# A decoder layer in 16 pipelined groups: one order table replaced by another, with begins of its own for each of six stages

## The reference

```python
h = rms_norm(x, g_pre)                                  # sublayer 1: gated recurrence
a = sigmoid(bit_linear(h, w_a) + decay_bias); i = sigmoid(bit_linear(h, w_i)); v = bit_linear(h, w_v)
rec = chunked_scan(a, sqrt(clip(1 - a*a, 1e-8)) * (i * v))      # state = a * state + input
x1 = layernorm(2*x + rec + bit_linear(silu(bit_linear(rms_norm(rec, g_post), w_gate)), w_down))
Q, K = rope(x1 @ Wq.T + bq), rope(ctx @ Wk.T + bk); V = ctx @ Wv.T + bv     # sublayer 2: 16 heads of 16
x2 = layernorm(x1 + softmax(where(mask == 0, min, Q @ K.T / 4)) @ V @ Wo.T + bo)
y = relu(s0 * concat(x2, -x2) @ (+-1)[k0]) * 2                  # sublayer 3: 512 -> 1024 -> 1024 -> 256
y = s2 * (relu(s1 * y @ (+-1)[k1]) * 2) @ (+-1)[k2]
out = layernorm(x2 + y)
```

## Time and profile before

| | |
|---|---|
| median of 3 runs | 890.84 us (889.0 to 891.39) |
| profiled execution | 888.45 us, of which its span is 886.7 us |
| PE busy | 800.9 us |
| DVE busy | 642.4 us |
| ACT busy | 549.2 us |
| POOL busy | 296.9 us |
| DMA | 57.47 MB, mean 65 GB/s |

### The profile page before, as it was taken

How to read it: one execution, slowest core, us unless ns; L and a number is a source line. 1 busy time by engine, 2 the same in 40 slices (tenths; PEclk the granted TensorE clock), 3 DMA queues, 4 the chain that set the end, 5 groups by cost and what they waited for, 6 DMA issues and landing times.

```text
span 886.7 us, 17907 instructions
## 1 busy us (share of the span) xinstructions
PE 800.9 (90%) x6856; PEld 626.3 (71%) x6890; DVE 642.4 (72%) x1224; ACT 549.2 (62%) x917; POOL 296.9 (33%) x476
## 2 busy tenths in 40 slices
...
DMA packets 52517, 57.47 MB, mean 65 GB/s; under 512 B 7856, under 2 KB 48848, under 8 KB 49360
## 3 DMA queue, kind: packets, MB, share of 16 engines
...
## 4 chain that ended last, share of the span: by engine, by line
PE 61%; DVE 16%; ACT 9%; DMA 4%; issue 4%; POOL 3%; SPq 1%; DVEq 0%; ACTq 0%; POOLq 0%
PE bankC L1118 18%; PE bankA L1053 6%; PE bankC L1102 6%; PE bankA L987 6%; PE slotB L1021 6%; PE slotB L1040 5%; PE bankA L922 5%; DMA q_st<-m_lo 4%; DVE u L1304 2%; ACT pr L794 2%; PE bankA L903 2%; DVE bn L1359 2%; ACT sqT L682 2%; ACT L794 2%; POOL rstd L574 2%
## 5 line engine op out<-in xcount | busy, mean ns | idle before, releaser
L1118 PE MATMUL bankC<-h0h,w 128*128 128x256 f16 x1024 | 233.7, 273 | 0.6 <-DVE h0l L1452 0.5
L1118 PE MATMUL bankC<-h0l,w 128*128 128x256 f16 x1024 | 233.3, 272 | 0.0
L1408 DVE TENSOR_REDUCE nmax<-slotB 128x4 f32<-128x1024 f32 x128 | 150.7, 1216 | 1.8 <-PE slotB L1021 0.3
L794 ACT ACTIVATE pr<-slotB 128x1024 f32<-128x1024 f32 x128 | 127.5, 1028 | 13.3 <-PE slotB L1040 13.0
L1118 PEld LDWEIGHTS bankC<-h0h,w 128*128 128x128 f16 x1024 | 99.9, 98 | 15.2 <-issue 1.2
L1118 PEld LDWEIGHTS bankC<-h0l,w 128*128 128x128 f16 x1024 | 100.1, 98 | 14.2
L1040 PE MATMUL slotB<-q_st,k_st 99*128 99x256 bf16 x512 | 74.7, 274 | 13.4 <-DMA q_st<-m_lo 11.2
L573 POOL TENSOR_SCALAR rstd<-mv 128x2 f32<-128x2 f32 x48 | 9.3, 193 | 215.6 <-DVE mv L1362 214.5
L1021 PE MATMUL slotB<-k_st,q_st 97*128 97x256 bf16 x512 | 76.7, 272 | 4.2 <-DVE nmax L1408 2.5
L1040 PEld LDWEIGHTS slotB<-q_st,k_st 99*128 99x128 bf16 x512 | 43.9, 97 | 38.3 <-DMA q_st<-m_lo 15.9
L1102 PE MATMUL bankC<-xh,w 128*128 128x256 f16 x256 | 57.8, 273 | 14.3 <-DVE xl L1446 13.7
...
## 6 DMA issues: line engine op xcount, KB each, us to landing
k_st<-scr SPq DMA_DIRECT2D x96, 128.0 KB, 4.5
q_st<-scr SPq DMA_DIRECT2D x96, 128.0 KB, 4.3
...
```

The costliest lines, as they stand in the source:

```text
L794: act.activation(pr[i % 2][:, c, :, :].rearrange("p h s -> p (h s)"), slotB[ringB.slot(g, name)][:, :], ACT.Exp, scale=DH ** -0.5).then_in ...
L1118: ins = pe.matmul(bankC[ringC.slot(g, name)][:, e * T:(e + 1) * T], w_1[:, i // 2, (2 * m + e) * P:(2 * m + e + 1) * P], (h0h, h0l)[i % 2] ...
L1408: dve.tensor_reduce(nmax[:, hg * HG * NT + n:(hg + 1) * HG * NT:NT], slotB[ringB.slot(g, name)][:, :].rearrange("p (h s) -> p h s", s=S), ...
```

## The change

The one table `TIMES` with the one list `BEGIN` becomes seven tables. Steps belong to `weights` or to one of six stages (recurrent, keys, queries, scores, values, network), each with its own list of begins; `when(step, engine, g)` takes the begin of the step's stage. From group 4 to group 12 all six lists advance by 47.87 in each group; in the first and the last groups they differ. Numbers of all steps are new, and with them the order on every engine and the places in the rings. No step's code, wait, buffer or DMA is changed: keys and queries still go to DRAM and back.

```diff
-TIMES = """
-    w:s V-601.472 P-451.567 | w:m V-188.378 A-211.738 P-145.016 | w:a V-131.916 | w:iv V-41.444
...
-BEGIN = [0, 53.194, 106.603, 159.927, 213.209, 266.528, 319.858, 373.172, 426.486, 479.8, 533.114, 586.428, 639.742, 693.116, 746.368, 799.574]
+TIMES = {
...
+    "scores": """
+        score0 P93.89 V95.551 | score1 P94.556 V101.441 | score2 P96.349 V103.898 | score3 P99.631 V104.717
...
+BEGIN = {
+    "weights": [0],
+    "recurrent": [0, 51.387, 91.429, 137.718, 185.585, 233.451, 281.317, 329.184,
+                  377.05, 424.917, 472.783, 520.649, 568.516, 616.394, 664.2, 712.324],
...
+    "scores": [0, 36.554, 83.319, 130.981, 178.847, 226.714, 274.58, 322.446,
+               370.313, 418.179, 466.046, 513.912, 561.778, 609.722, 657.92, 704.956],
...
 ENGINES = ("PE", "ACT", "DVE", "POOL", "SP")
...
+AT, BEGINS = times()
+
+
+def when(step, engine, g):
+    return BEGINS[step][g] + AT[step][engine]
 
 
 def order(engine):
 
-    steps = [(BEGIN[g] + at[engine], n, step, g)
-             for n, (step, at) in enumerate(AT.items()) if engine in at
-             for g in range(1 if step.startswith("w:") else G)]
+    steps = [(when(step, engine, g), n, step, g)
+             for n, (step, at) in enumerate(AT.items()) if engine in at for g in range(len(BEGINS[step]))]
     return [(step, g) for _, _, step, g in sorted(steps)]
...
-        for start, name, g in sorted((BEGIN[g] + AT[name]["PE"], name, g) for name in items for g in range(G)):
+        for start, name, g in sorted((when(name, "PE", g), name, g) for name in items for g in range(G)):
             engine, last = items[name]
             s = until.index(min(until))
             self.where[(name, g)] = (s, n[s])
-            until[s] = BEGIN[g] + AT[last][engine]
+            until[s] = when(last, engine, g)
             n[s] += 1
```

94 lines of the change are left out of this document (57 added, 37 removed).

## The result

The change makes the kernel 1.2% faster, by less than half of what was forecast: 880.88 us median (879.02 to 882.22) against 891.12 us for the kernel before, measured beside it; ratio 0.9878, 95% interval 0.9861 to 0.9896. The profiled execution took 882.22 us with a span of 880.3 us. Lines of the new program are those of the old plus 31.

A forecast was written before the change was run, and what follows sets the result against it. TensorE, 90% busy, was taken as the bound. Pitch 49.5 - 2.65 + 0.5 = 47.35 us gives 27.6 us less over 12.85 groups; fill +5.6, drain -5, together -27.0: 861.4 profiled, 864 median, range 849 to 882.

The forecast's parts named there:

- The three waits: TensorE's steady-part waits for xl, the row of maxima in q_st and sqT: 2.65 us a group, forecast to go.
- the drain: From l0_0(13) to l0_0(15): the old waits go there too, 5 us less, between 2 and 8.
- the last network: Group 15's network alone at the end, 31.0 us, same order in both kernels.
- rival 2: SyncE's queue delivers the row of maxima late in every group; at 6.5 us late about 920 us; chance 8%.
- One of the three readings: At sqT before down: only exp1.0 (0.44 us) stood between them in the old order; its 0.6 us wait goes.
- new small waits, 0.5 us: Steady part, each group: the new order's small delays cost 0.5 us, bounds 0 and 1.3.
- rival 1: VectorE becomes the bound between score0 and max: pitch 48.5 us, 880 us; chance 16%.
- the walk: One group followed through all five queues of the new order with the trace's durations; the fill was walked too.
- the ten places that come out 0.1 to 0.2 us late: Steps late in one steady group, x2T among them: 1.3 us added up, taken as 0.5.
- VectorE needs 18.9 us ... PE's order has 19.9 us: From score0 to max in each group: VectorE's work fits TensorE's matmuls with 0.3 us to spare.
- the fill, +5.6 us: Start until l0_0(0): the new order reaches it at 135.5 us, against 129.9 for equal work, 6 us either way.

The follow-up runs named there:

- Experiment 16: Changed kernel with GpSimd's rotk working on 8 of 256 columns from group 2 on, so keys are wrong: 868.78 us, ratio 0.9738 to the kernel before.
- 17: Changed kernel with round3's multiplication and rounding of sg on ScalarE instead of VectorE, whole computation: 870.54 us, ratio 0.9776 to the kernel before.
- experiment 3: Changed kernel with VectorE's maximum of xg (scale) behind x2 instead of ahead of the third maximum: 890.92 us, ratio 0.9998 to the kernel before.
- 4: Changed kernel with SyncE sending the query parts (qput) before gathering the key stack (kget): 911.97 us, ratio 1.024 to the kernel before.
- 8: Changed kernel with three of six key-stack gathers fetching one row instead of sixteen from group 2 on: 875.17 us, ratio 0.9824 to the kernel before.
- 10: Changed kernel with VectorE's two operations on the key parts ahead of layer 0's first low half: 887.68 us, ratio 0.9965 to the kernel before.
- 9: Changed kernel with the last low half of layer 1 behind x2 on VectorE: 895.71 us, ratio 1.006 to the kernel before.
- 11: Changed kernel with seven idle_work blocks left out and five added in earlier gaps of the fill: 876.88 us, ratio 0.9833 to the kernel before.
- 12: Changed kernel with layer 1's last low half behind x2, key parts ahead of layer 0's low half, and idle_work blocks moved: 896.79 us, ratio 1.0064.
- 15: Changed kernel with score5 later on PE, round3 ahead of score4's maximum, two maxima later on VectorE, and idle_work blocks moved: 880.0 us, ratio 0.9886.
- 14: Changed kernel with score5 later on PE, round3 ahead of score4's maximum and two maxima later on VectorE: 883.97 us, ratio 0.9937 to the kernel before.
- 18: Changed kernel with round3's multiplication on ScalarE and idle_work blocks moved in the fill, whole computation: 866.27 us, ratio 0.972 to the kernel before.
- 1: Changed kernel with each maximum reading only the first 128 of 256 keys: 869.96 us, ratio 0.9776 to the kernel before.
- 2: Kernel before, old order, with each maximum reading only the first 128 of 256 keys: 883.94 us, ratio 0.993 to the kernel before.
- 6: Changed kernel with x2T behind l2.2 and l2.3 and v ahead of the maxima on PE: 885.62 us, ratio 0.9936 to the kernel before.

## Why the prediction was off

**Right.** The three waits of the earlier trace rows are gone and came back nowhere as such. TensorE was the engine to follow, the drain gave 6.0 us for the 5 forecast, the last network took 30.9 us, and the row of maxima in SyncE's queue (rival 2) didn't decide. The direction was right. One of the three readings was wrong, though its wait went: between sqT and down the old order had not exp1.0 alone but also two quarter-steps of layer 1, 2.2 us in all and more than the new order's 1.75. What made sqT late was ScalarE's list, with a table load (1.28 us) and an exponential ahead of it, and that is what the new order took away:

```profile
440.17 1.28 ACT L794 ACT_TABLE_LOAD   x1 [1.88 <-PE slotB L1040]
441.46 1.02 ACT L794 ACTIVATE pr<-slotB 128x1024 f32<-128x1024 f32 x1
442.38 1.11 ACT L682 ACTIVATE sqT<-bankA,cst 128x1024 bf16<-128x1024 f16 x1
```

The time lies in the range of 849 to 882 us, 1.1 us from its end, and the forecast of 864 missed by 16.9.

**Wrong: the term "new small waits, 0.5 us".** It measured 1.54 us, over even its upper bound of 1.3; in 12.85 groups that is 13 us of the 17 missed. With it the pitch is 49.5 - 2.65 + 1.54 = 48.4, as measured, so the rest of that sum was right. The mechanism is that of rival 1, VectorE between score0 and max, which had been given 16%; its number (pitch 48.5, 880 us) fits by luck. Its own terms, 1.3 us and as much again, give 49.4, and the 0.9 that it then takes off comes from no row; and it had the fill at 5.6 us. x2T stood in the walk among the ten places that come out 0.1 to 0.2 us late; it waits 0.77. Two steps of the working failed.

First, the step "VectorE needs 18.9 us ... PE's order has 19.9 us". It took round3 at 1.25 us, its duration beside an idle GpSimd; in the new order it takes 0.69 + 0.17 + 1.58 = 2.44 us beside rotk. With these 1.2 us the step's own sum is 0.9 us short where it had 0.3 to spare. Experiment 16 takes the neighbour away, 17 the operations, and each brings back most of x2T's and score6's 1.22 us (to 0.36 and 0.60). That GpSimd's neighbourhood is the cause is shown by these two together; that it is the ports is only argued, with the rule of the Trainium skill named at experiment 16.

Second, the same step compared totals over 20 us. VectorE's idle time in that stretch lies at its start, where it waits for PE. What binds is the last part, 9.0 us without a gap from score4's maximum to x2 (experiment 3: work taken away ahead of it gives nothing). A margin of 0.3 us over the whole says nothing on such a part.

The remaining 0.32 us are score0's wait: q_st lands late. The prediction looked at this path for the drain alone, ahead of score0(15), with the loads' 4.3 us to landing; it isn't among the ten places of the steady part. The order puts qput right behind six key gathers, and its landing went from 2.7 to 5.3 us (experiments 4, 8 and 10). SyncE's list in the new order:

```profile
443.76 2.89 SPq L467 DMA_DIRECT2D k_st<-scr  x6
447.49 0.38 SPq L456 DMA_DIRECT2D scr<-qpart  x1
```

**Wrong: the fill, +5.6 us.** It measured +13.3, beyond the 6 us either way that it was given; in other executions of the same fill (experiments 9 and 4) it would be 12.4 and 11.2. Of these 6 to 8 us more, idle_work blocks that stood in the way or were missing explain a part: with the blocks moved, the fill lost 5.3, 4.2, 2.2 and 2.2 us less (11 against the new order, 12 against 10, 15 against 14, 18 against 17), of which up to 2 can be the spread between executions. How much of that is the clock and how much the blocks' own time was not separated. VectorE's maxima beside the work of groups 1 and 2 make the fill some 4 us more sensitive to their length than the old one (1 and 2), so what they add was underrated, but how much of it was in the walk's 5.6 stays open. The walk put score0(0) at 79, exp0.0(0) at 102 and l0_0(0) at 135.5; they came at 81.8, 105.3 and 142.5 us.

**What stays open.** Experiments 3, 4, 6, 9, 10 and 14 each moved one or a few numbers, took the wait they aimed at or put it elsewhere, and ended 3 to 31 us above the new order; their new waits are read from the traces, and what part of the time each of them makes was not separated. Whether an order exists that keeps rotk away from round3 without new waits wasn't tried. The parts of the fill beyond those above weren't either.
